# Attention-weighted pair products with an MLP tower: a part of the first tile's pairs is taken in eight steps of 16 samples before the other steps

## The chip, the cores and the metric

The kernel runs on one NeuronCore of a Trainium2 chip. The metric is device time in microseconds (us) of one execution; smaller is better. The time of a kernel is the median of its runs, and beside them one more execution was taken with the hardware profiler. In the profile the engines are PE (TensorE matmul), PEld (TensorE weight load, which overlaps PE), DVE (VectorE), ACT (ScalarE), POOL (GpSimd) and SP (SyncE, here a DMA queue).

## The reference

1024 samples, 33 embedding tables, rows of 128 values. With F = 33 there are 528 pairs of fields for each sample.

```python
e = jnp.stack([tbl_f[ids[:, f]] for f in range(33)], axis=1)     # (1024, 33, 128)
row, col = np.triu_indices(33, k=1)                              # 528 pairs
inner = e[:, row] * e[:, col]
fm = relu(einsum('bpd,ad->bpa', inner, attn_W) + attn_b)
scores = einsum('ba,bpa->bp', gnn_feature, fm)
attn = softmax(scores, axis=1)
attn_output = einsum('bp,bpd->bd', attn, inner) * 100.0
h = concatenate([gnn_feature, attn_output, gnn_feature], axis=1)
h = maximum(h @ W_top1 + b_top1, 0); h = maximum(h @ W_top2 + b_top2, 0)
y = h @ W_top3
```

## The kernel before, in words

The 1024 samples are T = 8 tiles of 128. A tile's 33 x 128 rows are gathered by 33 indirect DMAs on POOL, one a field (L280), into `x_rows`. They are turned by TensorE in five transposition jobs of 8, 8, 8, 8 and 1 fields (`transpose_x(t, c)`, L620), each evacuated by ACT into `xt` (`evacuate_xt`, L347), which then holds, for each of the 128 embedding dimensions, all fields of all samples. The first 16 fields are repeated behind field 32 (`repeat`, L337), so that a pair is a field and the field at distance 1 to 16 behind it in a ring of 33: 16 x 33 = 528 pairs. When all 33 fields are gathered, SP stores the rows to `x_dram` (L230), and only after that store do the gathers of the next tile begin; each also waits until its transposition job has read `x_rows`.

A tile is worked off in 32 steps of 4 samples (4 x 528 = 2112 columns). In one step
- DVE makes the products (`product(S)`, L418, one instruction of 2112 elements);
- the columns are cut into five chunks of 424 or 416. The first chunk (two in steps 2, 5, 8, 11, 14 and 17; four in step 0, three in step 1) goes "native" through TensorE in fp32 (L580, two records a chunk). The rest is split in high and low parts: ACT rounds the products (`round_inner`, L316), DVE subtracts (`rest_of_inner`, L423), and TensorE makes three fast matmuls a chunk (L587, L588, L589);
- ACT applies bias and relu to two chunks at a time (`relu`, L308) from a ring of three double PSUM banks into `fm` (three steps deep);
- after every second step TensorE reduces `fm` with the samples' gnn features into `scores` (`reduce_steps`, L610). These matmuls use 32 columns of the array each, so that the four samples of a step run side by side in four column groups; 16 matmuls of 264 columns for two steps, two records each, so 32 records, in eight rounds of four.

DVE runs ahead: `product(S + 3)` stands in its loop at step S. ACT rounds step S + 2 between its relus of step S. The order on each engine is written out by hand. Softmax, the weighted sums (`fields` jobs, L634) and the MLP of a tile come in the steps of the following tile; the transposition jobs of the next tile come after steps 18, 20, 22, 24 and 26.

For tile 0 there is nothing to do meanwhile. ACT copies all five jobs and makes both repeats, DVE then waits for all of it, and step 0 begins:

```python
dve.wait_ge(s_xt_out, XJ)
dve.wait_ge(s_repeat, K // FU)
product(0)
product(1)
rest_of_inner(0)
product(2)
```

Of the kernel before, what the change touches and what calls it, by code (L numbers as in the profile page):

```python
# [7 lines left out]
ALU = mybir.AluOpType  # L8
# [4 lines left out]
def afm_tower(nc, gnn, ids, tables, w1, b1, w2, b2, w3, attn_w, attn_b, out):  # L13
# [16 lines left out]
    assert EDGES[0][-1] == EDGES[1][-1] == COLS and ALL % 2 == 0  # L30
    H1, H2 = w1.shape[1], w2.shape[1]
# [13 lines left out]
    NATIVE[0], NATIVE[1] = 4, 3  # L45
    FIRST = 0
    SPLIT = COLS - min(EDGES[S % 2][NATIVE[S]] for S in range(ALL))
# [4 lines left out]
    XT_AT = (18, 20, 22, 24, 26)  # L52
    MLP_AT = (19, 21, 23)
# [10 lines left out]

    def jobs_of(S):
        t, s = divmod(S, STEPS)
        jobs = []
        if s in FIELDS_AT and t > 0:
            jobs.append(("fields", t - 1, FIELDS_AT.index(s)))
        if s in XT_AT and t + 1 < T:  # L70
# [8 lines left out]
    units = [("x_t", 0, c) for c in range(XJ)]  # L79
    for S in range(ALL):  # L80
        pair, odd = divmod(S, 2)
        units += [("hidden", pair, j) for j in ((3, 4) if odd else (0, 1, 2))] + jobs_of(S)
# [4 lines left out]
    with ctx:  # L87
# [93 lines left out]
        def slot(unit):  # L181
            return ring[place[unit] % RING]

        def taken_out(unit):

            kind, a, b = unit
            if kind == "hidden":
                return s_fm, SLOTS * a + b + 1
# [13 lines left out]
        def native_cols(S):  # L202
            return EDGES[S % 2][NATIVE[S]]

        def chunk_place(S, c):

            pair, odd = divmod(S, 2)
            j, h = divmod(CHUNKS * odd + c, 2)
            return slot(("hidden", pair, j)), h
# [85 lines left out]
        def _(act):  # L295
            def relu(pair, j):
                act.wait_ge(s_hidden, 2 * (SLOTS * pair + j + 1))
                S = 2 * pair
                if j == 0 and S >= FM_BUFS:
                    act.wait_ge(s_red, (S - FM_BUFS) // 2 + 1)  # L300
                if j == 2 and S + 1 >= FM_BUFS:
                    act.wait_ge(s_red, (S + 1 - FM_BUFS) // 2 + 1)
                n = THIN if j == 2 else WIDE
                at = [(S + c // CHUNKS) % FM_BUFS * COLS + EDGES[c // CHUNKS][c % CHUNKS] for c in (2 * j, 2 * j + 1)]
                first = fm[:, 0, 0:1]
                dst = bass.AP(tensor=first.tensor, offset=first.offset + at[0],
                              ap=[first.ap[0], [at[1] - at[0], 2], [1, n]])
                nc.scalar.activation(dst, slot(("hidden", pair, j))[:, :, 0:n], ACT.Relu,  # L308
                                     bias=attn_b_sb[:, 0:1]).then_inc(s_fm, 1)

            def round_inner(S):
                act.wait_ge(s_inner, S + 1)
                if S >= HI_BUFS:
                    act.wait_ge(s_hidden, CHUNKS * (S - HI_BUFS + 1))
                at = native_cols(S)
                nc.scalar.copy(inner_hi[:, S % HI_BUFS, 0:COLS - at], plain[:, S % INNER_BUFS, at:]).then_inc(s_hi, 1)  # L316
# [52 lines left out]
            for c in range(XJ):  # L369
                evacuate_xt(0, c)  # L370
                if c < K // FU:
                    repeat(0, c)
            round_inner(0)
            round_inner(1)
            for S in range(ALL):
                t, s = divmod(S, STEPS)
                relu(S // 2, 2 if S % 2 else 0)
                if part_at(S, EXP_AT) is not None:
                    exps(part_at(S, EXP_AT))
                if S + 2 < ALL:  # L380
# [3 lines left out]
                relu(S // 2, 3 if S % 2 else 1)  # L384
                if S % 2:
                    relu(S // 2, 4)
# [5 lines left out]
                if t + 1 < T and s - 1 in XT_AT[0:K // FU]:  # L392
                    repeat(t + 1, XT_AT.index(s - 1))
# [12 lines left out]
        def _(dve):  # L406
            def product(S):
                if S >= INNER_BUFS:
                    dve.wait_ge(s_hidden, CHUNKS * (S - INNER_BUFS + 1))
                t, s = divmod(S, STEPS)  # L410
                x = xt[:, t % 2, GROUPS * s:GROUPS * (s + 1), :]
                a = x[:, :, 0:F]
                part, sample, field = a.ap
                a = bass.AP(tensor=a.tensor, offset=a.offset, ap=[part, sample, [0, K], field])
                b = x[:, :, 1:1 + F]
                b = bass.AP(tensor=b.tensor, offset=b.offset, ap=[part, sample, [1, K], field])
                dst = plain[:, S % INNER_BUFS].rearrange("d (g k f) -> d g k f", g=GROUPS, k=K)
                nc.vector.tensor_tensor(dst, a, b, ALU.mult).then_inc(s_inner, 1)  # L418

            def rest_of_inner(S):  # L420
                dve.wait_ge(s_hi, split_steps(S))
                at, end = native_cols(S), COLS
                nc.vector.tensor_tensor(inner[:, S % INNER_BUFS, at:end], plain[:, S % INNER_BUFS, at:end],  # L423
                                        inner_hi[:, S % HI_BUFS, 0:end - at].bitcast(FP32), ALU.subtract).then_inc(s_lo, 1)
# [10 lines left out]
            def row_max(p):  # L435
                dve.wait_ge(s_red, PART_END[p] // 2)
                nc.vector.tensor_reduce(neg_max[:, 0:1], scores_v, AX.XY, ALU.max, negate=True).then_inc(s_max, 1)
# [127 lines left out]
        def _(pe):  # L565
# [5 lines left out]
            def hidden(S):  # L571
                pe.wait_ge(s_inner, S + 1)
                for c in range(CHUNKS):
                    begin, end = EDGES[S % 2][c:c + 2]
                    bank, h = chunk_place(S, c)
                    dst = bank[:, h, 0:end - begin]
                    if h == 0:
                        claim(("hidden", S // 2, (CHUNKS * (S % 2) + c) // 2))
# [16 lines left out]

            def reduce_steps(S0, last_pair=False):
# [3 lines left out]
                if s0 == 0:  # L600
                    pe.wait_ge(s_blocks, t + 1)
                pe.wait_ge(s_fm, SLOTS * (S0 // 2) + (3 if last_pair else SLOTS))
                for S in (S0, S0 + 1):
                    if last_pair and S > S0:
                        pe.wait_ge(s_fm, SLOTS * (S0 // 2 + 1))
                    s = S % STEPS
                    for h in range(2):
                        for j in range(GROUPS):
                            at = j * PAIRS + h * HALF
                            last = nc.tensor.matmul(scores[I * j:I * j + I, h, 0:HALF], block_of(s, j),  # L610
                                                    fm[:, S % FM_BUFS, at:at + HALF], start=s == 0, stop=s == STEPS - 1,
                                                    skip_group_check=True)
# [62 lines left out]
            for c in range(XJ):  # L675
                transpose_x(0, c)
            pe.wait_ge(s_zero, 3)
            for S in range(ALL):
# [8 lines left out]
                if S >= 2 and S % 2 == 0:  # L687
                    reduce_steps(S - 2)
# [33 lines left out]
```

## Time and profile before

| | |
|---|---|
| median of 3 runs | 1270.41 us (1270.02 to 1271.27) |
| the profiled execution | 1270.63 us |
| its span, first to last instruction | 1268.2 us |
| granted TensorE clock, mean | 1.000 |
| PE busy | 1201.0 us, 95% |
| DVE busy | 1147.9 us, 91% |
| ACT busy | 1018.7 us, 80% |
| POOL busy | 451.8 us, 36% |

Busy shares are means over the whole span. Where the kernel waits is read from stretches: the time before the first step, the 32 steps of tile 0, and the tiles after it.

### The profile page before, as it was taken

The page shows a single profiled execution, that of the slowest core. Times are in us where ns is not written, and L with a number is a line of the kernel's source. Part 1 is how long each engine was busy: PE and PEld are TensorE (multiplying, and loading weights), DVE is VectorE, ACT ScalarE, POOL GpSimd, SP SyncE. Part 2 cuts the span into 40 slices and gives each one's busy share as a digit, 9 for nine tenths or more (in the row PEclk, how much of TensorE's full clock was granted, in tenths as well). Part 3 has the DMA queues.
Part 4 walks back from the last instruction along what each step waited for, and adds up shares of the span by engine and source line. Part 5 has one row for each costly group of instructions (what it writes and reads, how often), then busy time and mean ns, then how long its engine had stood idle before and what let it go on. Part 6 is the DMA issues. An engine that isn't in the chain of part 4 may idle for free.

```text
span 1268.2 us, 20736 instructions
## 1 busy us (share of the span) xinstructions
PE 1201.0 (95%) x8732; PEld 898.7 (71%) x8732; DVE 1147.9 (91%) x649; ACT 1018.7 (80%) x1039; POOL 451.8 (36%) x270
## 2 busy tenths in 40 slices
PE   1499999999999999999999999999999999999998
PEld 1267676777777777777777777677777777777766
DVE  2399899998999989999899989999799998999994
ACT  1288898778987889878897798978888788887883
POOL 6587684018800386005840088201880000000000
PEclk9999999999999999999999999999999999999999
DMA  4211410311103111131101311031110300011001
GB/s 108 97 34 50 105 32 26 102 45 30 34 13 125 31 32 28 30 106 37 32 20 47 106 27 32 20 111 39 30 34 21 117 18 1 1 29 39 17 9 38
DMA packets 54859, 58.83 MB, mean 46 GB/s; under 512 B 10728, under 2 KB 49136, under 8 KB 53744
## 3 DMA queue, kind: packets, MB, share of 16 engines
q1 hardware_dynamic: 46304, 40.20, 10.4%
q0 software_dynamic: 8448, 17.32, 5.2%
q8 instruction: 69, 1.13, 0.4%
q14 instruction: 22, 0.18, 0.0%
q10 hardware_dynamic: 16, 0.00, 0.0%
HBM read 36.12 MB, written 17.31 MB: 42 GB/s over the span
## 4 chain that ended last, share of the span: by engine, by line
PE 83%; ACT 8%; issue 4%; DVE 2%; POOL 2%; another core or an unknown queue 1%; DMA 1%; SPq 0%; ACTq 0%; DVEq 0%; POOLq 0%
PE scores L610 19%; PE ring L580 17%; PE ring L587 13%; PE ring L589 12%; PE ring L588 12%; PE ring L634 4%; ACT fm L308 3%; ACT inner_hi L316 3%; PE ring L620 2%; POOL x_rows L280 2%; PE ring L654 1%; DVE products L418 1%; ACT exp_pairs L323 1%; PE ring L648 1%
## 5 line engine op out<-in xcount | busy, mean ns | idle before, releaser
L308 ACT ACTIVATE fm<-ring,attn_b_sb 128x848 f32<-128x848 f32 (+1 forms) x640 | 597.2, 971 | 183.1 <-PE ring L580 174.3
L418 DVE TENSOR_TENSOR products<-xt 128x2112 f32<-128x2112 f32 x256 | 601.9, 2351 | 37.1 <-ACT xt L347 37.1
L280 POOL DMA_INDIRECT x_rows<-in_tbl,ids_all x264 | 451.1, 1709 | 498.2 <-PE ring L620 408.3
L423 DVE TENSOR_TENSOR low_parts<-products,inner_hi 128x1688 fp32r<-128x1688 f32 (+4 forms) x256 | 467.1, 1825 | 57.1 <-ACT inner_hi L316 56.0
L587 PE MATMUL ring<-inner_hi,attn_wt_lo 128*128 128x424 f32 (+1 forms) x971 | 433.1, 446 | 5.1 <-ACT fm L308 5.1
L316 ACT CAST inner_hi<-products 128x1688 fp32r<-128x1688 f32 (+4 forms) x256 | 392.3, 1532 | 5.2 <-DVE products L418 5.2
L589 PE MATMUL ring<-inner_hi,attn_wt_hi 128*128 128x424 f32 (+1 forms) x971 | 344.1, 354 | 0.0
L588 PE MATMUL ring<-low_parts,attn_wt_hi 128*128 128x424 f32 (+1 forms) x971 | 343.7, 354 | 0.0
L580 PE MATMUL ring<-products,attn_wt 128*128 128x424 f32 (+1 forms) x618 | 275.8, 542 | 10.0 <-issue 6.4
L610 PE MATMUL scores<-fm,gnn_blocks 128*32 128x264 f32 x4096 | 254.6, 389 | 6.5 <-ACT exp_pairs L323 6.4
L587 PEld LDWEIGHTS ring<-inner_hi,attn_wt_lo 128*128 128x128 f32 x971 | 182.6, 188 | 70.8 <-issue 37.6
L588 PEld LDWEIGHTS ring<-low_parts,attn_wt_hi 128*128 128x128 f32 x971 | 183.0, 188 | 43.5 <-issue 40.1
L610 PEld LDWEIGHTS scores<-fm,gnn_blocks 128*32 128x32 f32 x4096 | 120.0, 109 | 107.7 <-issue 13.8
L589 PEld LDWEIGHTS ring<-inner_hi,attn_wt_hi 128*128 128x128 f32 x971 | 182.4, 188 | 5.2
L580 PEld LDWEIGHTS ring<-products,attn_wt 128*128 128x128 f32 x618 | 104.6, 190 | 85.4 <-issue 78.2
L620 PE MATMUL ring<-ident,x_rows 128*128 128x128 f32 x264 | 39.2, 292 | 34.0 <-DMA x_rows<-in_tbl,ids_all 31.1
L634 PE MATMUL ring<-attn_t,x_fields 128*128 128x128 f32 x512 | 62.5, 275 | 2.0 <-ACT attn_t L401 1.4
L634 PEld LDWEIGHTS ring<-attn_t,x_fields 128*128 128x128 f32 x512 | 61.8, 191 | 3.2 <-issue 3.1
L347 ACT COPY xt<-ring 128x1024 f32<-128x1024 f32 (+1 forms) x40 | 38.5, 964 | 31.3 <-PE ring L620 15.7
L620 PEld LDWEIGHTS ring<-ident,x_rows 128*128 128x128 f32 x264 | 33.0, 151 | 39.4 <-DMA x_rows<-in_tbl,ids_all 25.7
L473 DVE TENSOR_TENSOR attn<-ring,xt 128x1024 f32<-128x1024 f32 x30 | 36.6, 1220 | 2.8 <-PE ring L634 2.8
L481 DVE TENSOR_REDUCE pooled<-attn 128x32 f32<-128x1024 f32 x30 | 36.5, 1216 | 0.1
(53 smaller groups left out, 203.9 us busy)
## 6 DMA issues: line engine op xcount, KB each, us to landing
x_dram<-x_rows SPq DMA_DIRECT2D x8, 2112.0 KB, 6.6
x_fields<-x_dram SPq DMA_DIRECT2D x128, 128.0 KB
x_rows<-in_tbl,ids_all POOLq DMA_INDIRECT x264
attn_t<-attn_turned SPq DMA_DIRECT2D x124, 32.0 KB, 1.9
w_sb<-in_W_top SPq DMA_DIRECT2D x2, 512.0 KB
x_fields<-in_r_gnn_feature SPq DMA_DIRECT2D x1, 512.0 KB
h<-in_W_top SPq DMA_DIRECT2D x1, 256.0 KB
ids_all<-in_ids SPq DMA_DIRECT2D x1, 132.0 KB, 2.7
```

The lines of the kernel that those rows point to most:

```text
L280: nc.gpsimd.indirect_dma_start(out=x_rows[:, f, :], out_offset=None, in_=tables[f], in_offset=bass.IndirectOffsetOnAxis(ap=ids_all[:, t, f ...
L308: nc.scalar.activation(dst, slot(("hidden", pair, j))[:, :, 0:n], ACT.Relu, bias=attn_b_sb[:, 0:1]).then_inc(s_fm, 1)
L316: nc.scalar.copy(inner_hi[:, S % HI_BUFS, 0:COLS - at], plain[:, S % INNER_BUFS, at:]).then_inc(s_hi, 1)
L418: nc.vector.tensor_tensor(dst, a, b, ALU.mult).then_inc(s_inner, 1)
L423: nc.vector.tensor_tensor(inner[:, S % INNER_BUFS, at:end], plain[:, S % INNER_BUFS, at:end], inner_hi[:, S % HI_BUFS, 0:end - at].bitcast ...
L580: nc.tensor.matmul(dst, attn_wt[:], plain[:, S % INNER_BUFS, begin:end], start=True, stop=True)\
L587: nc.tensor.matmul(dst, attn_wt_lo[:], hi, start=True, stop=False)
L588: nc.tensor.matmul(dst, attn_wt_hi[:], lo, start=False, stop=False)
L589: nc.tensor.matmul(dst, attn_wt_hi[:], hi, start=False, stop=True).then_inc(s_hidden, 1)
L610: last = nc.tensor.matmul(scores[I * j:I * j + I, h, 0:HALF], block_of(s, j), fm[:, S % FM_BUFS, at:at + HALF], start=s == 0, stop=s == ST ...
L620: last = nc.tensor.transpose(to[:, n // 4, n % 4 * P:(n % 4 + 1) * P], x_rows[:, FU * c + n, :], ident[:])
L634: last = nc.tensor.matmul(bank[:, h, to:to + QS * I], x[:, n, :], own[:, :, n, :], start=True, stop=True)
```

## The change

Tile 0 alone is changed. Of its pairs, those of the fields 0 to 12 with the field 1 to 8 places behind (so among the fields 0 to 20; 13 x 8 = 104 of the 528 of a sample) are taken out of the 32 steps. They are done in eight steps numbered -8 to -1, of 16 samples and 16 x 104 = 1664 columns each, in four native chunks of 416. They need only the first three transposition jobs. The fourth and the fifth come on TensorE after the chunks of steps -6 and -5, the repeats on ACT after the relus of steps -4 and -3. The reduction of such a step is one matmul of 104 columns for each of its 16 samples, into the columns of `scores` that belong to these pairs; two steps make 32 matmuls, 64 records.

The steps 0 to 31 keep 424 pairs a sample: 1696 columns in four chunks of 424. The products are two DVE instructions (640 and 1056 elements). The reduction keeps its 16 matmuls for two steps, eight of 160 columns and eight of 264. Step 0 has three native chunks (four before), step 1 two (three before). From step 32 on nothing is changed.

```diff
+    AHEAD, AHEAD_K, AHEAD_SAMPLES = 13, 8, 16
+    BEGIN = -(P // AHEAD_SAMPLES)
+    AHEAD_PAIRS = AHEAD * AHEAD_K
+    NEAR = AHEAD_K * (F - AHEAD)
+    LEFT = GROUPS * (PAIRS - AHEAD_PAIRS)
...
-    NATIVE[0], NATIVE[1] = 4, 3
+    NATIVE[0], NATIVE[1] = 3, 2
+    def edges(S):
+        if S < 0:
+            return list(range(0, AHEAD_SAMPLES * AHEAD_PAIRS + 1, 4 * AHEAD_PAIRS))
+        if S < STEPS:
+            return list(range(0, LEFT + 1, LEFT // 4))
+        return EDGES[S % 2]
...
+    FIRST_XT_AT = {-6: 3, -5: 4}
+    FIRST_REPEAT_AT = {-4: 0, -3: 1}
...
# ACT
-            for c in range(XJ):
+            for c in range(3):
                 evacuate_xt(0, c)
-                if c < K // FU:
-                    repeat(0, c)
-            round_inner(0)
-            round_inner(1)
-            for S in range(ALL):
+            for S in range(BEGIN, ALL):
...
+                if S in FIRST_REPEAT_AT:
+                    repeat(0, FIRST_REPEAT_AT[S])
...
# DVE
+                if S < 0:
+                    pieces = [((S - BEGIN) * AHEAD_SAMPLES, AHEAD_SAMPLES, 0, AHEAD, 1, AHEAD_K)]
+                elif S < STEPS:
+                    pieces = [(GROUPS * S, GROUPS, AHEAD, F - AHEAD, 1, AHEAD_K), (GROUPS * S, GROUPS, 0, F, AHEAD_K + 1, K - AHEAD_K)]
+                else:
+                    pieces = [(GROUPS * (S % STEPS), GROUPS, 0, F, 1, K)]
...
-            dve.wait_ge(s_xt_out, XJ)
-            dve.wait_ge(s_repeat, K // FU)
-            product(0)
-            product(1)
-            rest_of_inner(0)
-            product(2)
-            for S in range(ALL):
+            dve.wait_ge(s_xt_out, 3)
+            for S in range(BEGIN, BEGIN + 3):
+                product(S)
+            for S in range(BEGIN, ALL):
                 t, s = divmod(S, STEPS)
-                if S + 1 < ALL:
+                if 0 <= S + 1 < ALL:
                     rest_of_inner(S + 1)
...
# TensorE
-                    if c < NATIVE[S]:
+                    if S < 0 or c < NATIVE[S]:
...
+            def scores_of(S):
+                near = [scores[I * j:I * j + I, 0, 0:HALF].rearrange("b (k f) -> b k f", f=F) for j in range(GROUPS)]
+                if S < 0:
+                    for i in range(AHEAD_SAMPLES):
+                        step, j = divmod((S - BEGIN) * AHEAD_SAMPLES + i, GROUPS)
+                        columns = fm[:, S % FM_BUFS, i * AHEAD_PAIRS:(i + 1) * AHEAD_PAIRS]
+                        yield step, j, step == 0, near[j][:, :, 0:AHEAD], columns.rearrange("p (k f) -> p k f", f=AHEAD)
+                    return
...
-            for c in range(XJ):
+            for c in range(3):
                 transpose_x(0, c)
             pe.wait_ge(s_zero, 3)
-            for S in range(ALL):
+            for S in range(BEGIN, ALL):
                 hidden(S)
...
-                if S >= 2 and S % 2 == 0:
+                if S >= BEGIN + 2 and S % 2 == 0:
                     reduce_steps(S - 2)
```

The units of the PSUM ring and the semaphore counts (`hidden_by`, `relus_by`, `pairs_of_steps`) are counted from step -8 on; they follow the same order. `product(0)` now waits for all five jobs and both repeats, as before.

## Rows read from the trace of the kernel before

**Rows 1.** Windows: busy us of each engine (instructions), granted clock, DMA share.

```profile
core 0: us, PE busy (x) PEld busy (x) DVE busy (x) ACT busy (x) POOL busy (x), PEclk, DMA share, GB/s
39.10:54.70 15.60, 2.18 (x9) 1.78 (x9) 2.41 (x2) 1.37 (x3) 5.19 (x7) 1.00 0.43 165
54.70:67.40 12.70, 12.31 (x38) 7.56 (x38) 12.70 (x8) 9.80 (x11) 11.46 (x5) 1.00 0.08 21
67.40:199.10 131.70, 129.92 (x962) 95.11 (x961) 125.64 (x63) 117.17 (x114) 102.93 (x58) 1.00 0.21 54
```

**Rows 2.** Timeline, 38 to 60 us: start, us, engine, operation, [idle before].

```profile
38.00 1.08 ACT L347 COPY xt<-ring 128x1024 f32<-128x1024 f32 x1 [7.68 <-PE ring L620]
...
46.19 2.18 PE L620 MATMUL ring<-ident,x_rows 128*128 128x128 f32 x9 [8.22 <-DMA x_rows<-in_tbl,ids_all]
47.43 0.34 SPq L230 DMA_DIRECT2D x_dram<-x_rows  x1
50.91 1.35 ACT L347 COPY xt<-ring 128x1024 f32<-128x1024 f32 x2 [11.83 <-remote]
52.29 4.63 DVE L418 TENSOR_TENSOR products<-xt 128x2112 f32<-128x2112 f32 x2 [37.07 <-ACT xt L347]
54.63 3.11 POOL L280 DMA_INDIRECT x_rows<-in_tbl,ids_all  x1 [8.88 <-DMA x_dram<-x_rows]
...
54.75 5.12 PE L580 MATMUL ring<-products,attn_wt 128*128 128x424 f32 x8 [6.38 <-issue]
...
59.38 0.68 PE L587 MATMUL ring<-inner_hi,attn_wt_lo 128*128 128x416 f32 x1
```

**Rows 3.** Chain that ended last, two reductions six pairs of steps apart.

```profile
75.61 1.92 PE scores L610 x32
...
125.06 1.92 PE scores L610 x32
```

**Rows 4.** PE timeline: first and last reduction of tile 0, one of tile 1.

```profile
67.39 1.99 PE L610 MATMUL scores<-fm,gnn_blocks 128*32 128x264 f32 x32
...
197.14 1.99 PE L610 MATMUL scores<-fm,gnn_blocks 128*32 128x264 f32 x32
...
347.12 1.99 PE L610 MATMUL scores<-fm,gnn_blocks 128*32 128x264 f32 x32
```

**Rows 5.** PE timeline inside one step, and a transposition job.

```profile
102.19 1.68 PE L580 MATMUL ring<-products,attn_wt 128*128 128x416 f32 x4
...
104.29 0.36 PE L587 MATMUL ring<-inner_hi,attn_wt_lo 128*128 128x424 f32 x1
...
104.87 0.36 PE L587 MATMUL ring<-inner_hi,attn_wt_lo 128*128 128x424 f32 x1
...
133.20 1.03 PE L620 MATMUL ring<-ident,x_rows 128*128 128x128 f32 x8
```

**Rows 6.** PE timeline cut at 100.5 and at 100.7 us.

```profile
100.28 0.43 PE L610 MATMUL scores<-fm,gnn_blocks 128*32 128x264 f32 x4
100.28 0.65 PE L610 MATMUL scores<-fm,gnn_blocks 128*32 128x264 f32 x8
```

**Rows 7.** Instructions of L610, 60 to 200 us: ns min/median/max.

```profile
L610 PEld LDWEIGHTS scores<-fm,gnn_blocks x512: 106/110/111, 67.4 to 198.5; 128*32 128x32 f32 x171
L610 PE MATMUL scores<-fm,gnn_blocks x512: 386/386/412, 67.4 to 198.7; 128*32 128x264 f32 x171
```

**Rows 8.** DVE timeline, 98 to 108 us.

```profile
98.40 1.48 DVE L423 TENSOR_TENSOR low_parts<-products,inner_hi 128x1272 fp32r<-128x1272 f32 x1
99.80 2.35 DVE L418 TENSOR_TENSOR products<-xt 128x2112 f32<-128x2112 f32 x1
102.07 1.91 DVE L423 TENSOR_TENSOR low_parts<-products,inner_hi 128x1688 fp32r<-128x1688 f32 x1
103.89 2.35 DVE L418 TENSOR_TENSOR products<-xt 128x2112 f32<-128x2112 f32 x1
```

**Rows 9.** ACT timeline, 105 to 110 us.

```profile
105.55 2.69 ACT L308 ACTIVATE fm<-ring,attn_b_sb 128x848 f32<-128x848 f32 x3
108.11 1.26 ACT L316 CAST inner_hi<-products 128x1264 fp32r<-128x1264 f32 x1
109.24 0.99 ACT L308 ACTIVATE fm<-ring,attn_b_sb 128x848 f32<-128x848 f32 x1
```

**Rows 10.** POOL timeline: gathers with DVE idle, then with DVE busy.

```profile
39.80 0.94 POOL L280 DMA_INDIRECT x_rows<-in_tbl,ids_all  x1 [0.30 <-issue]
...
44.80 0.94 POOL L280 DMA_INDIRECT x_rows<-in_tbl,ids_all  x1 [0.30 <-issue]
...
64.03 1.08 POOL L280 DMA_INDIRECT x_rows<-in_tbl,ids_all  x1 [0.30 <-issue]
...
121.12 1.96 POOL L280 DMA_INDIRECT x_rows<-in_tbl,ids_all  x1 [0.30 <-issue]
```

More of the change, by code:

```diff
@@ L44, in afm_tower, with chunks @@
     NATIVE = [2 if S % STEPS in NATIVE_2 else 1 for S in range(ALL)]
-    NATIVE[0], NATIVE[1] = 4, 3
+    NATIVE[0], NATIVE[1] = 3, 2
     FIRST = 0
-    SPLIT = COLS - min(EDGES[S % 2][NATIVE[S]] for S in range(ALL))
+    def edges(S):
[4 more added lines that the diff above has]
+        return EDGES[S % 2]
+    def chunks(S):
+        return len(edges(S)) - 1
+    SPLIT = max(edges(S)[-1] - edges(S)[NATIVE[S]] for S in range(ALL))
     INNER_BUFS, HI_BUFS, FM_BUFS = 4, 3, 3
@@ L69, in jobs_of @@
             jobs.append(("fields", t - 1, FIELDS_AT.index(s)))
-        if s in XT_AT and t + 1 < T:
+        if S in FIRST_XT_AT:
+            jobs.append(("x_t", 0, FIRST_XT_AT[S]))
+        if s in XT_AT and 0 < t + 1 < T:
             jobs.append(("x_t", t + 1, XT_AT.index(s)))
@@ L76, in jobs_of, with hidden_by, relus_by, pairs_of_steps @@
         return jobs
-    units = [("x_t", 0, c) for c in range(XJ)]
-    for S in range(ALL):
-        pair, odd = divmod(S, 2)
-        units += [("hidden", pair, j) for j in ((3, 4) if odd else (0, 1, 2))] + jobs_of(S)
+    CHUNK_LIST = [(S, c) for S in range(BEGIN, ALL) for c in range(chunks(S))]
+    CHUNK_NO = {chunk: n for n, chunk in enumerate(CHUNK_LIST)}
+    PAIR_OF = [CHUNK_LIST[n:n + 2] for n in range(0, len(CHUNK_LIST), 2)]
+    def hidden_by(S):
+        return CHUNK_NO[S, chunks(S) - 1] + 1
+    def relus_by(S):
+        return CHUNK_NO[S, chunks(S) - 1] // 2 + 1
+    def pairs_of_steps(S):
+        return (S - BEGIN) // 2
+    units = [("x_t", 0, c) for c in range(3)]
+    for S in range(BEGIN, ALL):
+        units += [("hidden", n, 0) for n, pair in enumerate(PAIR_OF) if pair[0][0] == S] + jobs_of(S)
     units += [("fields", T - 1, c) for c in (2, 3)] + [("mlp", T - 1, n) for n in range(3)]
@@ L571, in hidden @@
             def hidden(S):
[L572 to L576, printed above, removed]
+                pe.wait_ge(s_inner, S - BEGIN + 1)
+                for c in range(chunks(S)):
+                    begin, end = edges(S)[c:c + 2]
+                    n, h = chunk_place(S, c)
+                    dst = slot(("hidden", n, 0))[:, h, 0:end - begin]
                     if h == 0:
-                        claim(("hidden", S // 2, (CHUNKS * (S % 2) + c) // 2))
-                    if c < NATIVE[S]:
+                        claim(("hidden", n, 0))
+                    if S < 0 or c < NATIVE[S]:
                         nc.tensor.matmul(dst, attn_wt[:], plain[:, S % INNER_BUFS, begin:end], start=True, stop=True)\
@@ L594, in block_of @@
                 return gnn_blocks[:, j, at - s:at - s + STEPS]
+            def scores_of(S):
[6 more added lines that the diff above has]
+                    return
+                s = S % STEPS
+                for h in range(2):
+                    for j in range(GROUPS):
+                        if S < STEPS and h == 0:
+                            columns = fm[:, S % FM_BUFS, j * NEAR:(j + 1) * NEAR]
+                            yield s, j, False, near[j][:, :, AHEAD:F], columns.rearrange("p (k f) -> p k f", f=F - AHEAD)
+                            continue
+                        at = j * PAIRS + h * HALF if S >= STEPS else GROUPS * NEAR + j * HALF
+                        yield s, j, s == 0, scores[I * j:I * j + I, h, 0:HALF], fm[:, S % FM_BUFS, at:at + HALF]
             def reduce_steps(S0, last_pair=False):
@@ L599, in reduce_steps @@
                     pe.wait_ge(s_exp, PART_END.index(S0) + 1)
-                if s0 == 0:
-                    pe.wait_ge(s_blocks, t + 1)
-                pe.wait_ge(s_fm, SLOTS * (S0 // 2) + (3 if last_pair else SLOTS))
+                if S0 == BEGIN or s0 == 0:
+                    pe.wait_ge(s_blocks, max(t, 0) + 1)
+                pe.wait_ge(s_fm, relus_by(S0 if last_pair else S0 + 1))
                 for S in (S0, S0 + 1):
                     if last_pair and S > S0:
[L605 to L612, printed above, removed]
+                        pe.wait_ge(s_fm, relus_by(S))
+                    for s, j, first, to, columns in scores_of(S):
+                        last = nc.tensor.matmul(to, block_of(s, j), columns, start=first, stop=S % STEPS == STEPS - 1,
+                                                skip_group_check=True)
                 last.then_inc(s_red, 1)
@@ L674, in _ @@
             pe.wait_ge(s_weights, 96)
-            for c in range(XJ):
+            for c in range(3):
                 transpose_x(0, c)
             pe.wait_ge(s_zero, 3)
-            for S in range(ALL):
+            for S in range(BEGIN, ALL):
                 hidden(S)
```

77 lines of the change are left out of this document (38 added, 39 removed).

## The prediction

> **What bounds the kernel now.** I read the busy time by stretches first [rows 1]. From 67.4 us to the end of tile 0 at 199.1, PE is busy 129.9 of 131.7 us, DVE 125.6, ACT 117.2: PE sets the pace, DVE is close behind. In the 15.6 us from 39.1 to 54.7 PE works 2.2 us. That idle stretch is what the change can use. The timeline [rows 2] tells why it is there: the third transposition job has been copied at 38.00 + 1.08 = 39.08; the last two are transposed at 46.19, copied at 50.91, and the first products begin at 52.29 and reach PE at 54.75.
>
> The granted clock reads 1.00 throughout [rows 1], the level of 2.4 GHz, yet the first matmuls, after PE has been mostly idle, are slow [rows 2]: the four native chunks from 54.75 to 59.38 take 4.63 us, where later two take 1.42 (below). So there is a slow start of 4.63 - 2.84 = 1.8 us.
>
> Then the anchors [rows 4]: the first reduction starts at 67.39, the last of tile 0 at 197.14, and it ends 1.92 us later (the chain's share of it, [rows 3]) at 199.06. Tile 1's corresponding one starts at 347.12, 149.98 later. Nothing from step 32 on changes, so I sum up to the end of tile 0's last reduction and carry the difference to the end.
>
> **Unit costs.** Pairs of steps in tile 0 without jobs: (125.06 - 75.61) / 6 = 8.24 us [rows 3]. A split chunk is three matmuls: 104.87 - 104.29 = 0.58 us [rows 5]. A native chunk of 424 is 0.71: the two at 102.19 last 1.68 to the modelled end of the last; their records are issued 0.35 apart, so 1.42 for both, and 0.70 for 416 columns. Reduction: the second round of four matmuls ends 0.22 us after the first [rows 6], and eight rounds are (1.99 - 0.39) / 7 = 0.23 apart at most; I take 0.222, that is 264 columns at 0.84 ns, the same 0.84 ns a column as a native record (0.355 / 424). One pair is then 2 x (0.71 + 4 x 0.58) = 6.06, plus 0.075 for the second native chunks (four in these 14 steps), plus 8 x 0.222 = 1.78; the 0.3 left of 8.24 is what changing to and from a reduction and short waits cost.
>
> DVE: 1272 elements take 1.48, 1688 take 1.91, 2112 take 2.35 [rows 8], so 1.046 ns an element and 0.14 fixed, of which 0.06 remain from start to start (99.80 - 98.40 = 1.40 for 1272, and 102.07 - 99.80 = 2.27 for 2112). ACT: a relu about 0.90 from start to start (2.69 for three), rounding 1264 elements 1.13 (109.24 - 108.11) [rows 9].
>
> **The eight steps ahead.** The first product of 1664 elements starts at 39.1, takes 0.14 + 1.74 = 1.88, and PE begins at 41.1, that is 13.65 us earlier. From there PE has, in order:
> - the slow start, as before: 1.8;
> - 32 native chunks of 416: 22.3. Per step DVE needs 1.80, ACT 1.8, PE 2.8, so PE sets the pace;
> - the two transposition jobs, which were hidden in the wait and are now in PE's path: the warm job is 1.03 for eight [rows 5]; nine with the changes of mode 1.3;
> - four reductions of 64 records in 16 rounds. No row shows a round of 104 columns. From below, by columns: 104 x 0.84 = 0.087 a round, 1.4 for 16. From above, a round costs what it costs now whatever its width: 0.222, 3.55 for 16. Weight loads of these matmuls last 0.110 each and are started one round ahead [rows 7]; a round of 0.087 is shorter than that. The four loads of a round are started together, and I take 0.112 a round, the load's length, nearest to the lower end: 1.8, plus the 0.3 of a change, 2.1 each, 8.4 in all;
> - steps 0, 1 and 2 with three, two and two native chunks: 2.71 + 2.58 + 2.58 = 7.9.
>
> Sum: 41.1 + 1.8 + 22.3 + 1.3 + 8.4 + 7.9 = 82.8 for the start of the reduction of steps 0 and 1, which was at 67.39. So at this point the changed kernel is 15.4 us behind.
>
> **Steps 3 to 32.** Between the first and the last reduction of tile 0 lie 15 pairs. Each loses two split chunks (1.16) and, in its reduction, four of eight rounds shrink from 264 to 160 columns: 160 x 0.84 = 0.134 by columns, above the load's 0.110, so 4 x 0.088 = 0.35. 15 x 1.51 = 22.7 off, except that step 32 belongs to tile 1 and keeps its chunk: 0.6 back. 129.75 - 22.7 + 0.6 = 107.7. The jobs in these steps stay. The last reduction ends 1.92 - 0.35 = 1.57 after its start: 82.8 + 107.7 + 1.6 = 192.1, before 199.06: **7.0 us earlier**.
>
> The cover for this: DVE per pair now has 640 + 1056 + 1272 elements a step, 2968 x 1.046 + 3 x 0.06 = 3.29, 6.6 a pair, 6.4 with the smaller low parts of steps 5 to 17; PE has 8.24 - 1.51 = 6.73. ACT: 2 x (2 x 0.90 + 1.13) = 5.9. PE stays the bound, by only 0.1 to 0.3 a pair.
>
> **The join at step 0.** `product(0)` now waits for both repeats, the second behind the relus of step -3 on ACT. Step -3 ends on PE at 41.1 + 1.8 + 6 x 2.8 + 1.3 + 2 x 2.1 = 65.2; relu and repeat (about 1.1) let DVE start at 67.4 and finish at 69.3. PE wants step 0 at 65.2 + 2.8 + 2.1 + 2.8 = 72.9. Behind the wait on DVE stand product(1), the small rest of step 0, product(2); low parts of step 1 come by my count at 75, PE wants them after 77. Nothing on the path, with 3.6 us to spare.
>
> **Gathers.** The products now run while fields 28 to 32 are still being gathered. With DVE idle a gather is issued every 1.25 us, with DVE busy every (121.12 - 64.03) / 29 = 1.97 [rows 10]; the first three took 3.1 each (54.63 to 64.03) [rows 2, 10]. The fourth job has four gathers to go at 39.80. At 1.97 they end at 47.7, and PE started 1.7 us after a job's last issue (44.80 - 0.30 to 46.19) [rows 2, 10]: 49.4. PE comes to it after step -6 at 41.1 + 1.8 + 8.4 = 51.3. Hidden. The store goes from 47.4 to about 51.5, the next tile's gathers from 54.6 to 59; 33 of them at 1.97 end at 124, and the last is wanted after step 26, later than 150. No cost.
>
> **A rule weighed.** A reduction's four matmuls start so close together that all four, each of 0.39 to 0.41, fit in 0.43 us [rows 6]. The Trainium skill, TensorE: Matmul & The Clock Gate, section "Wait — 56ns, not 53.3ns?", says that with hardware decode off the sequencer spends about 62 ns on a MATMUL, which binds once the array's work is shorter. By that price a reduction ahead would be an estimated 64 x 0.062 = 4.0 us and not 1.8 (+8.8 for four), and a round of 160 columns in tile 0 0.25 and not 0.134 (+7.4 for 64 of them): about 1280. The rows here show 32 matmuls in 1.99 us all told, just at that price on average, but four at once within a round, so they don't settle it; rival A is that mechanism at the price of the rows.
>
> **Rivals.**
> A. Narrow matmuls cost what wide ones do (a fixed price a round, here 0.222, 0.056 a matmul). For it: no row shows a narrow one, and 64 pairs of load and matmul must be supplied. Against it: four start within 0.02 us. Ahead 4 x 1.76 = +7.0; in tile 0 the 0.35 is not won, 16 x 0.35 = +5.6. Together +12.6: 1276.0, slower. It decides for a loss once a round of 104 or 160 columns costs more than 0.18 us.
> B. The start-up hits PE. Before, the copy waited from 48.2 (last transposition) to 50.91 for a signal from outside [rows 2], 2.5 us; in the new order the same stall would stand in PE's path. Or the gathers run at 3.1 us as just after 54.63 [rows 2, 10]: fourth job ready at 39.8 + 12.5 + 1.7 = 54.0, PE waits 2.7. Either: 1266.0; both 1268.6.
> C. DVE becomes the bound in tile 0, if shorter runs (20 elements) or the third instruction cost more: each 0.1 us a step beyond the 0.1 to 0.3 a pair of slack is 3 us. 1265 to 1268.
> D. Rounds by columns alone (0.087): 4 x 0.4 = -1.6, and smaller changes of mode: 1259 to 1262.
>
> **The numbers.** The profiled execution took 1270.63; less 7.0 is 1263.6. The median of the runs is 0.2 lower: 1263.4. Under 0.2% (2.5 us) a measurement of this kernel can hardly tell from none. Chances: my forecast (1261.5 to 1265.5) 0.40, D 0.10, B 0.20, C 0.14, A 0.16. Faster by over 0.2% (under 1267.9): the forecast, D, B with one of its two delays (0.14), the smaller half of C (0.08): 0.72. Within 0.2%: B with both, the rest of C, and A where a round costs 0.18 to 0.20: 0.06 + 0.06 + 0.04 = 0.16. Slower: the rest of A, 0.12. The range of 1258.5 to 1272.5 leaves out that end of A and the lower end of D with shorter changes of mode.
>
> **What the new profile would show.** First native matmul at 41.1; reductions of 64 records of 2.1 us (A: 3.8); fourth job's transpositions near 51.3 with no wait before; the first reduction of tile 0 with 32 records at 82.8 and the last near 190.5; pairs of 6.7 us between; tile 1 unchanged at 149.98. Wrong would be: records ahead spaced evenly at 0.05 us or more; PE waiting for DVE's low parts in steps 3 to 31; slow matmuls again after 46 us.

## The result and the profile after

The changed kernel takes 1300.08 us (median of 5 runs, 1299.14 to 1301.99) against 1270.41 (by now five runs too, 1270.02 to 1271.39); the ratio is 1.0235, 95% interval 1.0221 to 1.0249. It is 30 us slower where 7 us faster were forecast. The profiled span is 1299.7 us, before it was 1268.2.

In the rows of the changed kernel L619 is a native chunk, L665 a reduction, L674 a transposition job, L345 a relu, L384 a copy of transposed fields, L374 a repeat and L318 a gather. A "count" below is the step that a finished instruction adds to its semaphore; the engine that waits for it goes on when it sees it.

The busy time by stretches (columns as in [rows 1]) shows the loss in one place:

```profile
core 0: us, PE busy (x) PEld busy (x) DVE busy (x) ACT busy (x) POOL busy (x), PEclk, DMA share, GB/s
60.00:76.00 16.00, 11.89 (x91) 6.22 (x89) 1.89 (x1) 5.11 (x6) 12.54 (x12) 1.00 0.19 49
76.00:94.00 18.00, 3.14 (x4) 1.17 (x4) 0.00 (x0) 0.95 (x1) 13.53 (x15) 0.53 0.19 51
94.00:98.00 4.00, 0.00 (x0) 0.00 (x0) 0.00 (x0) 0.00 (x0) 3.09 (x4) 0.92 0.25 63
98.00:111.00 13.00, 6.65 (x69) 4.38 (x70) 6.40 (x7) 4.21 (x5) 2.25 (x3) 0.50 0.67 210
111.00:122.00 11.00, 11.00 (x98) 7.33 (x96) 7.26 (x8) 8.78 (x10) 0.00 (x0) 1.00 0.39 65
```

From about 73 to 101 us TensorE, VectorE and ScalarE stand nearly still together: PE runs four records, VectorE none from 63.84 to 101.69, ScalarE two relus. Only POOL works: it issues the gathers of tile 1. PE has stood idle since 72.9 when the granted clock falls: it reads 0.61 from 76 to 80 us and its lower level, 0.50, from 80 to 92.

The PE timeline of the changed kernel (start, us, [idle before]), which answers to [rows 2, 4]:

```profile
43.63 7.39 PE L619 MATMUL ring<-products,attn_wt 128*128 128x416 f32 x12 [5.71 <-issue]
52.03 4.46 PE L619 MATMUL ring<-products,attn_wt 128*128 128x416 f32 x12 [1.01 <-ACT fm L345]
...
57.29 1.64 PE L665 MATMUL scores<-fm,gnn_blocks 128*32 128x104 f32 x64
...
64.75 1.89 PE L665 MATMUL scores<-fm,gnn_blocks 128*32 128x104 f32 x55
66.99 0.40 PE L665 MATMUL scores<-fm,gnn_blocks 128*32 128x104 f32 x6 [0.36 <-issue]
67.75 0.38 PE L665 MATMUL scores<-fm,gnn_blocks 128*32 128x104 f32 x3 [0.36 <-issue]
68.07 0.97 PE L619 MATMUL ring<-products,attn_wt 128*128 128x416 f32 x2
69.22 3.65 PE L619 MATMUL ring<-products,attn_wt 128*128 128x416 f32 x10 [0.19 <-issue]
90.14 3.14 PE L619 MATMUL ring<-products,attn_wt 128*128 128x416 f32 x4 [17.27 <-issue]
100.64 1.27 PE L665 MATMUL scores<-fm,gnn_blocks 128*32 128x104 f32 x24 [7.36 <-ACT fm L345]
105.22 0.33 PE L665 MATMUL scores<-fm,gnn_blocks 128*32 128x104 f32 x1 [3.31 <-issue]
...
122.07 1.64 PE L665 MATMUL scores<-fm,gnn_blocks 128*32 128x160 f32 x32
...
227.33 1.64 PE L665 MATMUL scores<-fm,gnn_blocks 128*32 128x160 f32 x32
```

Two things are to be seen. The first reduction ahead runs in one piece, 64 records in 1.64 us. The second breaks up at its end: its last records come a few at a time with "issue" between, that is, PE waits for nothing that the profile shows. And the four chunks of step -3 have run by 71.5 us (two records at 68.07, the first six of the ten from 69.22, 0.35 apart), but ScalarE takes the first two out only at 89.13 and the other two at 99.63. The chain of waits of the changed kernel (start, us, what) says the same:

```profile
64.86 0.95 ACT fm L345
65.81 1.02 ACT xt L374
66.83 16.64 another core or an unknown queue
83.47 0.02 issue
...
83.51 5.60 another core or an unknown queue
89.11 0.02 issue
89.13 0.95 ACT fm L345
90.08 9.52 another core or an unknown queue
```

Where the chain knows no releaser, the semaphore's count came long after the matmul that carries it. L338 is ScalarE's wait for a reduction: that of steps -6 and -5 ran by 68.2 and counted at 83.47, 15 us late. The first two chunks of step -3 ran by 70.1 and counted by 89.11, 19 us late; the other two ran by 71.5 and ScalarE, which waits for nothing else there, took them at 99.63, 28 us late. A smaller stretch of the same kind stands at the start, in ScalarE's timeline:

```profile
40.52 1.08 ACT L384 COPY xt<-ring 128x1024 f32<-128x1024 f32 x1 [11.47 <-remote]
51.02 3.67 ACT L345 ACTIVATE fm<-ring,attn_b_sb 128x832 f32<-128x832 f32 x4 [9.42 <-PE ring L619]
```

The third transposition job, copied at 38.00 before [rows 2], is copied at 40.52, and the first relu comes at 51.02 though two chunks have run by about 46.7. POOL meanwhile, from 64.97 us on at its quickest pace, 0.94 and 0.30 between:

```profile
66.22 0.94 POOL L318 DMA_INDIRECT x_rows<-in_tbl,ids_all  x1 [0.30 <-issue]
67.46 0.94 POOL L318 DMA_INDIRECT x_rows<-in_tbl,ids_all  x1 [0.30 <-issue]
...
99.91 0.95 POOL L318 DMA_INDIRECT x_rows<-in_tbl,ids_all  x1 [0.30 <-issue]
```

Before the change, gathers followed each other at this pace for long only before the first step; those of tile 1 ran beside a busy VectorE, one in 1.97 us [rows 10].

### The profile page after: what moved, and what is told of

It reads as the page before. It is cut to its first block, busy times and chain, and to the rows that moved or that the text cites. A ratio compares the mean times of both kernels' runs of the same rounds, so it can differ in the third digit from the quotient of the medians.

```text
span 1299.7 us, 21251 instructions
## 1 busy us (share of the span) xinstructions
PE 1211.9 (93%) x8958; PEld 901.3 (69%) x8958; DVE 1138.1 (88%) x689; ACT 1009.7 (78%) x1039; POOL 419.2 (32%) x270
## 4 chain that ended last, share of the span: by engine, by line
PE 79%; ACT 7%; DVE 5%; issue 4%; another core or an unknown queue 2%; POOL 2%; DMA 0%; ACTq 0%; DVEq 0%; POOLq 0%
PE scores L665 18%; PE ring L619 18%; PE ring L626 12%; PE ring L628 11%; PE ring L627 11%; PE ring L688 4%; ACT fm L345 3%; ACT inner_hi L353 2%; PE ring L674 2%; DVE products L459 2%; POOL x_rows L318 2%; DVE low_parts L465 2%; PE ring L708 1%; ACT exp_pairs L360 1%
## 5 line engine op out<-in xcount | busy, mean ns | idle before, releaser
L345 ACT ACTIVATE fm<-ring,attn_b_sb 128x848 f32<-128x848 f32 (+1 forms) x640 | 599.4, 972 | 234.8 <-PE ring L619 182.3
L459 DVE TENSOR_TENSOR products<-xt 128x2112 f32<-128x2112 f32 (+3 forms) x296 | 605.1, 2054 | 72.0 <-issue 37.8
L318 POOL DMA_INDIRECT x_rows<-in_tbl,ids_all x264 | 418.5, 1585 | 562.7 <-PE ring L674 472.8
L465 DVE TENSOR_TENSOR low_parts<-products,inner_hi 128x1696 fp32r<-128x1696 f32 (+5 forms) x256 | 454.0, 1774 | 64.2 <-ACT inner_hi L353 62.9
L626 PE MATMUL ring<-inner_hi,attn_wt_lo 128*128 128x424 f32 (+1 forms) x941 | 422.3, 449 | 5.7 <-ACT fm L345 4.5
L353 ACT CAST inner_hi<-products 128x1696 fp32r<-128x1696 f32 (+5 forms) x256 | 381.9, 1492 | 0.7 <-DVE products L459 0.7
L628 PE MATMUL ring<-inner_hi,attn_wt_hi 128*128 128x424 f32 (+1 forms) x941 | 333.5, 354 | 0.0
L627 PE MATMUL ring<-low_parts,attn_wt_hi 128*128 128x424 f32 (+1 forms) x941 | 333.2, 354 | 0.0
L619 PE MATMUL ring<-products,attn_wt 128*128 128x424 f32 (+1 forms) x678 | 302.6, 547 | 27.8 <-issue 23.2
L665 PE MATMUL scores<-fm,gnn_blocks 128*32 128x264 f32 (+2 forms) x4352 | 258.7, 378 | 18.6 <-ACT fm L345 7.4
L626 PEld LDWEIGHTS ring<-inner_hi,attn_wt_lo 128*128 128x128 f32 x941 | 177.0, 188 | 70.1 <-issue 38.0
L665 PEld LDWEIGHTS scores<-fm,gnn_blocks 128*32 128x32 f32 x4352 | 127.2, 110 | 118.0 <-issue 21.0
L619 PEld LDWEIGHTS ring<-products,attn_wt 128*128 128x128 f32 x678 | 117.2, 193 | 115.0 <-issue 103.6
L674 PE MATMUL ring<-ident,x_rows 128*128 128x128 f32 x264 | 38.3, 287 | 23.8 <-DMA x_rows<-in_tbl,ids_all 22.4
L384 ACT COPY xt<-ring 128x1024 f32<-128x1024 f32 (+1 forms) x40 | 38.7, 967 | 24.8 <-PE ring L674 13.3
L674 PEld LDWEIGHTS ring<-ident,x_rows 128*128 128x128 f32 x264 | 32.2, 148 | 29.2 <-DMA x_rows<-in_tbl,ids_all 16.7
```

Source lines behind the costliest of these rows:

```text
L318: nc.gpsimd.indirect_dma_start(out=x_rows[:, f, :], out_offset=None, in_=tables[f], in_offset=bass.IndirectOffsetOnAxis(ap=ids_all[:, t, f ...
L345: nc.scalar.activation(dst, slot(("hidden", n, 0))[:, :, 0:wide], ACT.Relu, bias=attn_b_sb[:, 0:1]).then_inc(s_fm, 1)
L353: nc.scalar.copy(inner_hi[:, S % HI_BUFS, 0:end - at], plain[:, S % INNER_BUFS, at:end]).then_inc(s_hi, 1)
L459: last = nc.vector.tensor_tensor(dst, a, b, ALU.mult)
L626: nc.tensor.matmul(dst, attn_wt_lo[:], hi, start=True, stop=False)
L627: nc.tensor.matmul(dst, attn_wt_hi[:], lo, start=False, stop=False)
```

## The experiments

Where a ratio stands, the time is a median of four to six executions; where none stands, it is that of a single one. The kernel before took 1268.8 to 1271.6 us in all executions beside them, so single times a few us apart prove little, and the traces carry those readings.

**Four kernels on what delays TensorE.** Theory G: POOL's gathers at full pace do. Theory R: the dense reductions do. Theory J: the transposition jobs four and five, done late, and the repeats do.

```diff
# e1: gathers of tile 1 late
             for t in range(T):
+                if t == 1:
+                    pool.wait_ge(s_inner, 1 - BEGIN)
                 gather(t)
```

> The changed kernel, but POOL issues the 33 gathers of tile 1 only after the products of step 0 (one wait on s_inner added). In the changed kernel's trace TensorE's chunks of step -3 run at 68 to 70 us, but their signals come at 86 to 106 us, while POOL issues gathers every 1.25 us with VectorE idle. Theory G (gathers at full pace hold TensorE's signals back): no such delay before step 0, first 32-record reduction near 80 us in place of 119, time 1264 to 1270. Theory R (the dense reductions of 128 short TensorE instructions outrun its supply of instructions, and the delay follows from that): unchanged, 1298 to 1302. Theory J (the late fourth and fifth jobs and the repeats are what hangs): unchanged too.

Measured: 1266.66 us, ratio to the kernel before 0.9963 (0.9951 to 0.9976). Two rows are ScalarE's, the last is PE's:

```profile
42.79 1.08 ACT L386 COPY xt<-ring 128x1024 f32<-128x1024 f32 x1 [13.69 <-remote]
51.20 1.80 ACT L347 ACTIVATE fm<-ring,attn_b_sb 128x832 f32<-128x832 f32 x2 [7.33 <-PE ring L621]
```

```profile
87.78 1.65 PE L667 MATMUL scores<-fm,gnn_blocks 128*32 128x160 f32 x32
```

The long delay is gone: the first tile-0 reduction starts at 87.78 instead of 122.07, though later than the 80 that I expected, since the delay at the start remains, a little longer. The gathers are needed for the 30 us; the reductions and the late jobs, which are all still there, don't bring it about alone.

```diff
# e2: a quarter of the reductions ahead
-                    for i in range(AHEAD_SAMPLES):
+                    for i in range(GROUPS):
```

> The changed kernel with a quarter of the reductions ahead: only 4 of the 16 samples of a step ahead are reduced (8 matmuls for two steps in place of 32), the rest of that work is left out. Theory R: the delay at 68 to 106 us is gone, time about 1262. Theory G: gathers run as before at that time, the delay stays (it may begin a few us earlier), 1292 to 1300.

Measured: 1262.05 us, for a kernel that leaves out three quarters of the reductions ahead and so of the scores of these pairs. PE timeline:

```profile
57.42 0.56 PE L665 MATMUL scores<-fm,gnn_blocks 128*32 128x104 f32 x16
...
70.08 0.56 PE L665 MATMUL scores<-fm,gnn_blocks 128*32 128x104 f32 x16
...
82.16 1.64 PE L665 MATMUL scores<-fm,gnn_blocks 128*32 128x160 f32 x32
```

The gathers were not changed (six from 64.02 to 70.28 follow at 1.25 us), and the long delay didn't come. So my theory G, gathers alone, falls as well: the long delay needs both the gathers at full pace and the many records of the reductions. (VectorE also waits less here, which slows the later gathers; the run doesn't separate the two.) The start, where no reduction has run yet, was delayed as before (first relu at 51.15).

```diff
# e3: gathers of tile 1 spaced
                         ).then_inc(s_gather[c], 16)
+                        if t == 1:
+                            nc.gpsimd.memset(slow[:], 0.0).then_inc(s_slow, 1)
+                            pool.wait_ge(s_slow, f + 1)
```

> The changed kernel with a memset of 512 elements on POOL behind each gather of tile 1, which spaces them by about 2 us instead of 1.25, as they are spaced in the kernel before. Theory G, if it is the pace that counts: no or a short delay, 1263 to 1275. Theory G, if any gathering with VectorE idle does it: the delay lasts as long as the gathers, 66 us, so 1320 or more. Theory R: unchanged near 1300.

Measured: 1266.19 us. The gathers run from 56.7 us on, in the same place as in the changed kernel, but one in 1.76 us or more. It is the pace that counts. The second reduction still shows one short break:

```profile
64.62 1.70 PE L670 MATMUL scores<-fm,gnn_blocks 128*32 128x104 f32 x60
66.67 0.40 PE L670 MATMUL scores<-fm,gnn_blocks 128*32 128x104 f32 x4 [0.36 <-issue]
```

```diff
# e4: all five jobs first
-            for c in range(3):
+            for c in range(XJ):          # transpose_x and evacuate_xt
-    FIRST_XT_AT = {-6: 3, -5: 4}
+    FIRST_XT_AT = {}
-            dve.wait_ge(s_xt_out, 3)
+            dve.wait_ge(s_xt_out, XJ)
```

> The changed kernel with all five transposition jobs before step -8, as in the kernel before, so that the steps ahead gain no start: they begin at about 52 us. Theory J: the delay is gone, first 32-record reduction near 92 us, time about 1273. Theory G: gathers of tile 1 begin at 54.6 and run at 1.25 us whenever VectorE waits in the steps ahead, so the delay of TensorE's signals comes again and ends some us after the last gather near 100 us: 1290 to 1300. Theory R: the delay comes too.

Measured: 1302.01 us. With jobs four and five out of the way the delay comes as before, PE idle until 97.60:

```profile
76.19 4.46 PE L619 MATMUL ring<-products,attn_wt 128*128 128x416 f32 x12
97.60 3.14 PE L619 MATMUL ring<-products,attn_wt 128*128 128x416 f32 x4 [16.95 <-ACT fm L345]
```

So the late jobs are not the cause, nor is the start with three jobs. The repeats were not moved here; but e1 and e3 have them where they were, and no long delay. (The time lies 2 us above the 1290 to 1300 that I gave for theory G.)

**Four on the start, and on the runs of short matmuls.** e5 and e6 contain the edit of e1 too.

```diff
# e5: gathers of fields 24 to 32 of tile 0 held
+                    if t == 0 and c == 3:
+                        pool.wait_ge(s_hidden, 2)
```

> The changed kernel with tile 1's gathers late (after the products of step 0), and with the gathers of fields 24 to 32 of tile 0 held until TensorE has signalled its first two chunks of step -8. No gather is then issued from about 34.5 us on. In the kernels run so far the third transposition job ends at 38.0 but is copied only at 40.4 to 42.8, and the first chunks of step -8, run from 43.6 on, are signalled at 51. Theory G for the start too (gathers hold TensorE's signals back while it waits): copy at 38.0, first relu near 44, both signals on time; then the fourth job comes late (gathers from 43 to 55), time about 1266 to 1269. Against it: copy again at 40 to 43 and first relu at 50 or later.

Measured: 1272.26 us. ScalarE's timeline:

```profile
37.98 1.08 ACT L388 COPY xt<-ring 128x1024 f32<-128x1024 f32 x1 [8.97 <-PE ring L678]
44.23 0.95 ACT L349 ACTIVATE fm<-ring,attn_b_sb 128x832 f32<-128x832 f32 x1 [5.18 <-PE ring L623]
```

With no gather issued from 34.4 to 44.5 us both counts come on time, 7 us earlier at the first relu than in e1. The total is later than the 1266 to 1269 expected: TensorE then waits for the fourth job's rows until 59.5 us, 8 us idle, and the mean granted clock of 60 to 70 us is 0.74.

```diff
# e6: those gathers spaced instead of held
                         ).then_inc(s_gather[c], 16)
+                        if t == 0 and c > 2:
+                            nc.gpsimd.memset(slow[:], 0.0).then_inc(s_slow, 1)
+                            pool.wait_ge(s_slow, f - FU * 3 + 1)
```

> The changed kernel with tile 1's gathers late, and the gathers of fields 24 to 32 of tile 0 spaced to about 2 us by a memset behind each. If the pace is what counts at the start as well: third job copied at 38.0, first relu near 44, first 32-record reduction near 82 in place of 87.8, time 1260 to 1263. If any gathering holds the signals back: as with tile 1's gathers late alone, 1266, or later by the 6 us that the last gathers are later.

Measured: 1261.04 us, ratio 0.9933 (0.9917 to 0.9950). The first row is ScalarE's, the others PE's:

```profile
38.31 1.08 ACT L391 COPY xt<-ring 128x1024 f32<-128x1024 f32 x1 [8.90 <-PE ring L681]
```

```profile
41.41 10.40 PE L626 MATMUL ring<-products,attn_wt 128*128 128x416 f32 x24 [3.14 <-issue]
...
52.61 1.64 PE L672 MATMUL scores<-fm,gnn_blocks 128*32 128x104 f32 x64
...
81.66 1.65 PE L672 MATMUL scores<-fm,gnn_blocks 128*32 128x160 f32 x32
...
186.90 1.64 PE L672 MATMUL scores<-fm,gnn_blocks 128*32 128x160 f32 x32
...
196.04 1.99 PE L672 MATMUL scores<-fm,gnn_blocks 128*32 128x264 f32 x32 [1.06 <-ACT exp_pairs L367]
```

This kernel runs as the prediction described. It is faster than the one before and the changed one, and by 5.6 us than that of e1, which is the price of the delay at the start (4.8 if each is taken against the kernel before that ran beside it; e8 below, which ran beside e6, gives 5.6 again).

```diff
# e7: reductions ahead after every step
-                if S >= BEGIN + 2 and S % 2 == 0:
+                if S >= BEGIN + 2 and S < 2:
+                    reduce_ahead(S - 2)
+                elif S >= 2 and S % 2 == 0:
                     reduce_steps(S - 2)
```

Each of these reductions is 16 matmuls, 32 records; a second semaphore tells the even steps.

> The changed kernel with the reductions ahead done after every step (32 matmuls, 64 TensorE instructions at a time) instead of after every second (128 at a time); gathers as in the changed kernel. If a long run of short TensorE instructions is what starts the delay (theory R as the trigger): no delay or a short one, 1264 to 1270. If only their number counts, not how they are grouped: 1295 to 1305.

(The number of matmuls in this text should be 16; 64 instructions counts a weight load and a matmul for each record.) Measured: 1293.84 us. Three runs of 32 records pass in 0.92 us each; the fourth breaks up:

```profile
68.61 1.29 PE L677 MATMUL scores<-fm,gnn_blocks 128*32 128x104 f32 x28
70.20 0.25 PE L677 MATMUL scores<-fm,gnn_blocks 128*32 128x104 f32 x1 [0.31 <-issue]
70.94 0.37 PE L677 MATMUL scores<-fm,gnn_blocks 128*32 128x104 f32 x3 [0.49 <-issue]
```

The delay comes 4 us later than in the changed kernel and costs nearly as much. Splitting the runs is no cure: the 1264 to 1270 of theory R were missed by far, the other figure, 1295 to 1305, by a little. What e2 took away was three quarters of the records; e7 took away only their grouping.

> The same with tile 1's gathers late as well. Both triggers away: 1266 to 1268, the time of tile 1's gathers late alone, plus at most 4 x 0.3 us for four more changes between chunks and reductions.

(The edits of e1 and e7 together.) Measured: 1266.61 us, ratio 0.9967 (0.9955 to 0.9980), the same as e1. With tile 1's gathers late it makes no difference how the reductions are grouped.

**Four on what it is in a gather.** e9 and e10 are e6 with something else in the place of tile 1's gathers.

```diff
# e9
+                    for i in range(60):
+                        nc.gpsimd.memset(slow[:, 0:128], 0.0).then_inc(s_slow, 1)
+                        pool.wait_ge(s_slow, F - FU * 3 + i + 1)
```

> The kernel with the last gathers of tile 0 paced and those of tile 1 late (1261 us), with 60 short memsets on POOL in the place where the changed kernel issues tile 1's gathers, 52 to 70 us. If a busy POOL (its instructions, or its port to the memory) is what holds TensorE's signals back: signals late, 1268 to 1290. If it is the gathers' transfers or their issue: unchanged, 1259 to 1263.

Measured: 1261.54 us, unchanged. POOL's timeline:

```profile
52.89 15.70 POOL L337 MEMSET slow<- 128x128 f32 x60
```

```diff
# e10
+            for f in range(F):
+                if f > 3:
+                    sp.wait_ge(s_spare[f % 4], 16 * (f // 4))
+                sp.dma_start(spare[:, f % 4, :], x_dram[0:P, f, :]).then_inc(s_spare[f % 4], 16)
```

> The same kernel, with 33 plain loads from the SP queue, each of 128 rows of 512 bytes as a gather has, after tile 0's store (about 58 to 75 us), into a spare tile. If the transfers and their semaphore counts are what holds TensorE back: signals late, a stretch of 10 to 20 us of slow reductions, 1268 to 1285. If it takes POOL's own way of issuing a gather: 1259 to 1264.

Measured: 1261.17 us, unchanged, with 33 transfers of a gather's size in 20.6 us, twice as dense as POOL's gathers:

```profile
61.84 20.64 SPq L289 DMA_DIRECT2D spare<-x_dram  x33
```

So neither a busy POOL alone nor as many transfers of this size from another queue do it. Of what was tried, only the indirect gathers issued by POOL do. Whether it is the indirect addressing, POOL's way of issuing a transfer or the two together, no run separates: plain transfers issued by POOL were not tried.

e11 and e12 are the changed kernel with nothing held, and a memset of 16 or of 512 elements behind each gather of fields 24 to 32 of tile 0 and of all of tile 1 (`if (t, c) in PACED`, otherwise as e6).

> The changed kernel with a memset of 16 elements behind each gather of fields 24 to 32 of tile 0 and of tile 1 (and POOL's wait for it): issues every 1.5 us or so instead of 1.25, nothing held. If a small gap is enough: third job copied at 38.3, no delay, 1260 to 1263. If the spacing has to be near 2 us: delays at the start or at 66 us, 1266 to 1290.

Measured: 1279.91 us. The memsets were shorter than I had reckoned, so the spacing was 1.35 us (66.99 - 65.64) and not 1.5, and reductions broke up again (the first rows are POOL's, the last is PE's):

```profile
65.64 0.95 POOL L324 DMA_INDIRECT x_rows<-in_tbl,ids_all  x1 [0.27 <-issue]
66.60 0.13 POOL L330 MEMSET slow<- 128x16 f32 x1
66.99 0.95 POOL L324 DMA_INDIRECT x_rows<-in_tbl,ids_all  x1 [0.27 <-issue]
```

```profile
64.96 0.41 PE L675 MATMUL scores<-fm,gnn_blocks 128*32 128x104 f32 x6 [0.32 <-issue]
```

> The changed kernel with a memset of 512 elements behind each of the same gathers, nothing held: about 1.8 us spacing, as with the paced kernels before. Expected as with tile 1's gathers late and tile 0's last ones paced: 1260 to 1262.

Measured: 1261.62 us, ratio 0.9940 (0.9923 to 0.9956), as expected, with a gather in 1.76 us (66.09 - 64.33) or more. From 1.25 over 1.35 to 1.76 us of spacing, the times are 1300, 1280 and 1262.

## Why the prediction was wrong

**The step that failed** is the one on the gathers: "Hidden. [...] No cost". I asked only when a gather's rows land and when they are wanted, and put what the gathers do to another engine at nothing, without a reason. I also took 1.97 us a gather for all 33 of tile 1, though my own sum has VectorE waiting in the steps ahead; they went at (99.91 - 56.73) / 32 = 1.35. VectorE waits in the steps ahead and at the join, so POOL is no longer slowed, and issues most of tile 1's gathers in 1.25 us instead of 1.97 [rows 10], just while TensorE has its many short reductions. TensorE's instructions then come a few at a time, and its counts up to 28 us late. The others wait for these counts, so VectorE stands idle, so the gathers stay at full pace until the last is out at 100.9: the delay keeps itself alive, as I read the traces. e1, e3, e6 and e12 show the cause by taking away the pace or the place; e2 shows that the many reductions are needed for the long delay.

**Rival B had the wait at the start, at half its price.** It put the 2.5 us wait of before for a signal into PE's path. The two delays of the start, at the third job's copy and at the first relu, cost about 5 us together (e1 and e8 against e6). That e1, at 1266.66, lies beside rival B's 1266.0 is luck: the delay is twice as dear, and the rest 2.4 us quicker than forecast (1261.04 for 1263.4). And nothing in the prediction let it return in the middle: the first tile-0 reduction is at 122.07 in the changed kernel, at 87.78 in e1 (34.3 less) and at 81.66 in e6 (6.1 less again). I had the row of before with "remote" and 11.83 us before me [rows 2] and priced it as a one-off, with no question as to what else was going on: POOL had been issuing at full pace until just before.

**The rest of the sum nearly holds**, by e6, which differs from the changed kernel by the times of its gathers alone (and the memsets that space them):

- PE's first chunk: forecast 41.1, there 41.41 (changed kernel 43.63).
- A reduction ahead: forecast 1.8 with 0.3 of change; 64 records take 1.64, of which 0.28 is the tail of the last round, so a round is 1.36 / 15 = 0.091 (0.114 for the first, 0.089 for the others), near the columns' price (rival D's 0.087), not the weight load's 0.112. From its start to the next chunk a reduction takes 52.61 to 54.17, 1.56 for a forecast of 2.1. Rival A, 0.222 a round, falls. The Trainium skill, TensorE: Matmul & The Clock Gate, section "Wait — 56ns, not 53.3ns?", gives about 62 ns a MATMUL with hardware decode off. The trace does not bear that price out for this kernel: 60 records in 1.36 us are 23 ns each, and two records counted as one matmul 45.
- A round of 160 columns: x32 takes 1.65 instead of 1.99 [rows 4], 0.34 less for a forecast of 0.35.
- First tile-0 reduction: forecast 82.8, there 81.66. The four cheaper reductions give 2.1; the start and the chunks take back 1.0.
- From the first to the last: forecast 107.7, measured 105.24 (in the changed kernel 227.33 - 122.07 = 105.26). The pairs without jobs are as forecast, near 6.75. Two pairs with transposition jobs, which took 10.50 and 10.15 before, take 7.54 each; together they gain 2.6 more than the sum's 1.51 each; in the kernel before PE stood idle for 1.8 us of them (busy 9.49 and 9.39), and now for none. The sum had kept that wait.
- The join at step 0: nothing on the path in e6, as forecast. Rival C, VectorE as the bound, did not come in tile 0: the pairs would be above 6.75.
- Tile 1 unchanged: not quite. In the changed kernel the same reduction of tile 1 starts at 378.87, 151.54 after 227.33, where it was 149.98. The 1.56 us are lost in the steps 5 to 8 of tile 1, in e6 as well, where VectorE is busy throughout; it comes out of tile 0 with less of a lead, which is my reading and no run isolates it.
- The sum: e6 is 10.2 us ahead at the start of tile 0's last reduction, 0.3 more at its end, and 9.0 at the end of the span (1268.2 to 1259.2). The forecast was 7.0: 1.1 came before the first reduction, 2.5 in the pairs, and tile 1 took 1.6 back.

**Not settled** is the mechanism inside the chip. No view shows why gathers that POOL issues every 1.25 us keep TensorE from its instructions and its counts late, when memsets on POOL and plain loads from SP don't. The Trainium skill, SBUF — State Buffer, section "Who interferes with whom", has it that a DMA never contends with a compute engine. e10 agrees for loads from SP; POOL's gathers do hold TensorE back in the changed kernel, though nothing here says that the memory's ports are the place. Why the counts of the start are late without any reduction (copy at 40.52, relu at 51.02), when those of the same transpositions were on time before, is open as well. And the pace of the moment is not all of it: the last two gathers before that relu start at 44.65 and 46.44, 1.8 us apart, and the counts of chunks run from 45 us on still come only at 51, after the last gather. How many short records it takes, between e2's 64 and the changed kernel's 256, was not tried.

## What to carry to other kernels

- An engine that is slowed by another is a brake with a use. When a change lets VectorE wait, ask what POOL will then do faster, and who suffers; here a saving of 9 us became a loss of 30.
- A row "remote" or "another core or an unknown queue" on this one-core program was a late signal. Find what ran at full pace beside it before pricing it as fixed.
- To keep an overlap and lose the collision, space the gathers (a memset of 512 elements behind each, 0.5 us on an idle POOL): 1261.6 us here (e12), 8 us under the kernel before. Or start tile 1's when VectorE is busy again and space only the last of tile 0: 1261.0 (e6), 9 us under.

## What the runs showed of the hardware

- Indirect gathers issued by POOL every 1.25 us, with VectorE mostly idle, hold back TensorE: its short instructions come in groups with 0.2 to 3.3 us between, and its semaphore counts come up to 28 us late. At 1.35 us it is milder (1280 us, one run), at 1.76 us all but gone (1262; one break of 0.36 us in e3). The long delay also needs the many short matmuls of the reductions: with a quarter of them it does not come (e2). 60 memsets on POOL in 15.7 us and 33 loads from SP in 20.6 us have no such effect.
- Matmuls of 32 columns of the array, four side by side, go at 0.84 to 0.86 ns per streamed column from 264 down to 104 columns (a round in 0.222 and 0.089 us), although the weight load of each is recorded as 0.110 us.
